# A four-layer graph network on one core: layer 0's first transfers, its softmax totals and its mark flips moved

## The reference, cut to what matters

```python
scores = jnp.einsum('hnd,hmd->hnm', q, k)
scores = jnp.where(adj > 0, scores, NEG_FILL)
attn = jax.nn.softmax(scores, axis=-1)
out = jnp.einsum('hnm,hmd->hnd', attn, vv)
...
x = _layernorm(x + _L0_gnn_ref(x, L0_gnn_x2, L0_gnn_v, adj), axis=-1)
```

## Time and profile before

| What | us |
|---|---|
| Three runs, median (lowest, highest) | 784.59 (783.59, 786.24) |
| The profiled execution's own time | 784.18 |
| Its span | 782.5 |
| TensorE busy in the span | 726.0 |
| VectorE busy | 657.7 |
| ScalarE busy | 545.3 |
| Mean granted TensorE clock, share of full | 0.984 |

### The profile page before, as it was taken

One profiled execution on the slowest core, in us unless ns is written; L12 is line 12 of the kernel. 1 busy time (PEld: TensorE's weight loads), 2 busy tenths in 40 slices (PEclk: granted clock), 3 DMA queues, 4 the chain that ended last, 5 costly groups with the idle time before them and its releaser, 6 DMA issues. The chain is left out here.

```text
span 782.5 us, 22935 instructions
## 1 busy us (share of the span) xinstructions
PE 726.0 (93%) x9908; PEld 454.3 (58%) x9908; DVE 657.7 (84%) x1001; ACT 545.3 (70%) x588; POOL 112.1 (14%) x220
## 2 busy tenths in 40 slices
PE   4798999999999999998889999999966999999996
PEld 1232333333333333336679999999963577776885
DVE  4797999999999999977899999999985757664544
ACT  7898999999999998773699999999904411111000
POOL 1421100310000000004310000000002323321222
PEclk9999999999999999999999999999996999999999
DMA  9998635363545451003271111101005000000001
GB/s 344 247 240 203 173 95 137 89 142 96 136 96 136 98 109 22 2 15 111 53 271 56 57 56 55 41 21 57 3 2 216 1 1 1 2 1 0 28 28 54
DMA packets 42599, 68.39 MB, mean 87 GB/s; under 512 B 4032, under 2 KB 27200, under 8 KB 40832
## 3 DMA queue, kind: packets, MB, share of 16 engines
q1 hardware_dynamic: 32976, 60.08, 25.3%
q0 software_dynamic: 9520, 6.82, 5.2%
HBM read 52.60 MB, written 10.09 MB: 80 GB/s over the span
## 5 line engine op out<-in xcount | busy, mean ns | idle before, releaser
L624 ACT ACTIVATE ex<-scores_ps,joint_shift 128x1024 f32<-128x1024 f32 x256 | 266.7, 1121 | 18.0 <-PE scores_ps L454 17.9
L707 DVE TENSOR_TENSOR esum<-esum,ex 128x1024 f32<-128x1024 f32 x188 | 217.2, 1216 | 1.2 <-ACT ex L624 1.2
L451 PE MATMUL scores_ps<-qst,kst 64*64 64x512 f16 x2048 | 158.7, 385 | 9.0 <-ACT ex L624 9.0
L1480 ACT ACTIVATE steps<-a_all,big_b_head 128x2048 fp8e5<-128x2048 f32 x86 | 163.6, 1988 | 0.0
L1195 PE MATMUL banks<-fx,pos 128*128 128x132 f16 x2048 | 159.4, 221 | 3.9 <-DVE pos L1387 3.7
L470 PE MATMUL mixed_total_ps<-ex,v 128*32 128x512 f32 x1024 | 125.6, 609 | 1.8 <-DMA v<-in_v_dram 1.8
L1195 PEld LDWEIGHTS banks<-fx,pos 128*128 128x128 fp8e5 x2048 | 120.6, 97 | 4.6 <-DVE pos L1387 2.6
L451 PEld LDWEIGHTS scores_ps<-qst,kst 64*64 64x64 f16 x2048 | 48.4, 106 | 116.0 <-ACT ex L624 84.7
L1202 PE MATMUL banks<-fm,edge 128*128 128x66 f16 x2048 | 103.7, 193 | 0.0
L454 PE MATMUL scores_ps<-masks,negI 64*64 64x512 bf16 x1024 | 99.8, 379 | 0.0
L1202 PEld LDWEIGHTS banks<-fm,edge 128*128 128x128 fp8e5 x2048 | 86.1, 97 | 0.0
(11 more groups left out here) (222 smaller groups left out, 722.9 us busy)
## 6 DMA issues: line engine op xcount, KB each, us to landing
adj_raw<-in_adjT_dram SPq DMA_DIRECT2D x32, 512.0 KB, 4.5
qst<-pieces_dram SPq DMA_DIRECT2D x28, 256.0 KB, 5.1
a_all<-score_rows_dram SPq DMA_DIRECT2D x7, 1024.0 KB, 6.6
edge<-masks POOLq DMA_DIRECT2D x32, 128.0 KB, 4.7
edge_copy_dram<-edge SPq DMA_DIRECT2D x1, 4096.0 KB, 17.1
edge_second<-edge_copy_dram SPq DMA_DIRECT2D x1, 4096.0 KB, 12.7
pieces_dram<-high_low SPq DMA_DIRECT2D x14, 256.0 KB, 4.2
ex<-in_x2T_dram SPq DMA_DIRECT2D x2, 1024.0 KB, 8.1
```

What stands on the lines that cost most here:

```text
L451: nc.tensor.matmul((one, two)[x][at], keys[rows, x, :], qst[rows, it % 2, half, 2 * p + x, :], start=(half == 0), stop=False, skip_group_c ...
L624: nc.scalar.activation(ex[:, slot(s), 2 * p:2 * p + 2, at], scores_ps[:, u % SR, :].rearrange("p (x n) -> p x n", n=CW), ACT.Exp, bias=joi ...
L707: nc.vector.tensor_tensor(esum[:, heads, at], other, ex[:, slot(s), heads, at], ALU.add).then_inc(summed, 1)
L1480: nc.scalar.activation(steps[:, pair_of(h, k) % SLOTS, jt % GU, :], aall[:, e, :], ACT.Relu, bias=bigh[:, e, jt:jt + 1], scale=BIG, satura ...
```

## The change

Five things. Totals: `add_halves` is gone; `total` reads the full width, eight matmuls instead of four, waits for the last additions of the round, and stands in step 8k, behind the mixing and ahead of the fourth score. Closing pieces: 0 and 1 in step 8k, 2 to 4 in the three after. Splits for later rounds: high part one step earlier, low part first in its step. Flips: all 16 behind VectorE's last additions, none in layer 1, and no waits on them there. First transfers: SP waits for the first half of `v` before x2 and x of the second group; SP's order within a step is store, load, stack; the second half of `v` comes at step 4 as one load and four swapped ones; `edge` stores begin at step 5; VectorE makes three low parts before the squares.

```diff
@@ -125,9 +125,12 @@
     JOBS = [("k", 0, 0), ("q", 0, 0), ("k", 0, 1), ("k", 0, 2), ("k", 0, 3), ("q", 1, 0), ("k", 1, 0), ("k", 1, 1),
             ("k", 1, 2), ("k", 1, 3), ("q", 0, 1), ("q", 1, 1), ("q", 0, 2), ("q", 1, 2), ("q", 0, 3), ("q", 1, 3)]
     FIRST = 5
-    SPLIT_AT = {2: 5, 3: 6, 5: 7, 7: 8, 8: 9, 9: 10, 17: 11, 25: 12, 33: 13, 41: 14, 49: 15}
+    SPLIT_AT = {2: 5, 3: 6, 5: 7, 7: 8, 8: 9, 9: 10, 16: 11, 24: 12, 32: 13, 40: 14, 48: 15}
+    LOW_AT = {s + (s >= 2 * JP): j for s, j in SPLIT_AT.items()}
     STEP_OF = {j: s for s, j in SPLIT_AT.items()}
     CONVERT_AT = {(m, t): m - 2 if m < JP else 2 * m + t - 10 for m in range(2, CONVERTED) for t in range(2)}
+    EDGE_AT = [max(m + 5, CONVERT_AT.get((m, 1), 0) + 1) for m in range(CONVERTED)]
+    SECOND_V_AT = 4
     CONVERTS = [[n for n in CONVERT_AT if CONVERT_AT[n] == s] for s in range(STEPS)]
 
     def round_of(c, g):
@@ -137,7 +140,7 @@
         what, g, c = JOBS[j]
         return JP * (round_of(c, g) - 1) - 1 if what == "q" and c else -1
 
-    STORE_AT = {j: STEP_OF[j] + 1 for j in STEP_OF}
+    STORE_AT = {j: s + 1 for s, j in LOW_AT.items()}
     STACK_AT = {j: max(STEP_OF[j], free_after(j)) + 2 for j in STEP_OF}
     LOAD_AT = {j: STEP_OF[j] - 2 for j in STEP_OF}
...
@@ -297,6 +300,7 @@
                 load_x(1)
                 for m in range(AHEAD):
                     load_adj(m)
+                sp.wait_ge(v_landed[0], 16)
                 load_x(2)
                 load_x(3)
                 for m in range(AHEAD):
@@ -309,11 +313,13 @@
                         for m, t in CONVERTS[s - 1]:
                             if t and m + AR < CONVERTED:
                                 load_adj_after(m)
-                    for j in range(3, len(JOBS)):
-                        if LOAD_AT.get(j) == s:
+                    for j in STORE_AT:
+                        if STORE_AT[j] == s:
+                            store_pieces(j)
+                    for j in LOAD_AT:
+                        if LOAD_AT[j] == s:
                             load_natural(j)
-                        if STORE_AT.get(j) == s:
-                            store_pieces(j)
+                    for j in STACK_AT:
                         if STACK_AT[j] == s:
                             stack(j)
...
@@ -349,19 +355,11 @@
                     for to, of in ((LO, HI), (HI, LO)):
                         pool.dma_start(vt[to, g, :, at], of_v[of]).then_inc(v_landed[g], 16)
 
-                def load_first_v():
-                    pool.dma_start(vt[:, 0], tiles(v)[:, :, 0:GW]).then_inc(v_landed[0], 16)
-                    pool.wait_ge(v_landed[0], 16)
+                def load_v(g):
+                    pool.dma_start(vt[:, g], tiles(v)[:, :, g * GW:(g + 1) * GW]).then_inc(v_landed[g], 16)
+                    pool.wait_ge(v_landed[g], 16)
                     for h in range(1, HG, 2):
-                        load_swapped(0, h)
-
-                def load_second_v():
-                    for h in range(HG):
-                        if h % 2:
-                            load_swapped(1, h)
-                        else:
-                            at, of = slice(h * DH, (h + 1) * DH), slice(GW + h * DH, GW + (h + 1) * DH)
-                            pool.dma_start(vt[:, 1, :, at], tiles(v)[:, :, of]).then_inc(v_landed[1], 16)
+                        load_swapped(g, h)
 
                 def keep_edges(m):
                     c, jp = m // JP, m % JP
...
-                load_first_v()
-                for m in range(AHEAD):
-                    keep_edges(m)
+                load_v(0)
                 for s in range(STEPS + 8):
-                    if s == 2:
-                        load_second_v()
-                    if 0 < s <= STEPS:
-                        for m, t in CONVERTS[s - 1]:
-                            if t:
-                                keep_edges(m)
+                    if s == SECOND_V_AT:
+                        pool.wait_ge(exp_ready, s * UNITS)
+                        load_v(1)
+                    for m in range(CONVERTED):
+                        if EDGE_AT[m] == s:
+                            if s <= STEPS:
+                                pool.wait_ge(exp_ready, s * UNITS)
+                            keep_edges(m)
                     if s == RANGE_AT + 2:
                         range_of_weights()
...
                         pe.wait_ge(shift_kept, 1)
                     if s % JP == 0 and it < G:
-                        pe.wait_ge(v_landed[it], 16 * (1 + HG, 3 * HG // 2)[it])
+                        pe.wait_ge(v_landed[it], 16 * (1 + HG))
                     for t in range(2):
                         jt = 2 * jp + t
                         for h in range(HG):
@@ -474,14 +472,16 @@
                     last.then_inc(mixed, 1)
 
                 def total(it):
-                    pe.wait_ge(halved, (it + 1) * PAIRS)
+                    pe.wait_ge(summed, (it + 1) * ADDS)
                     if it:
                         pe.wait_ge(recip_step, (it - 1) * CLOSING + 1)
                     if it == SUM_AT // JP:
                         pe.wait_ge(w_ready, KT)
-                    for h in range(HG):
-                        last = nc.tensor.matmul(total_ps[h * DH:(h + 1) * DH, :], ones[:, 0:DH], esum[:, h, 0:CW],
-                                                start=True, stop=True)
+                    for t in range(2):
+                        for h in range(HG):
+                            last = nc.tensor.matmul(total_ps[h * DH:(h + 1) * DH, :], ones[:, 0:DH],
+                                                    esum[:, h, t * CW:(t + 1) * CW], start=(t == 0), stop=(t == 1),
+                                                    skip_group_check=True)
                     last.then_inc(totals, 1)
...
                         for i in range(UNITS - 1):
                             score(s, i)
-                    if s > JP and s % JP == 1:
-                        total(s // JP - 1)
                     if s == STEPS:
                         last_total(esum, True)
                     if s:
                         mix(s - 1)
+                    if s and s < STEPS and s % JP == 0:
+                        total(s // JP - 1)
                     if s < STEPS:
                         score(s, UNITS - 1)
...
                 step = Chain(dve, top_step)
                 keep_shift(0)
-                make_low(2)
-                square(0)
-                for j in range(3, FIRST):
+                for j in range(2, FIRST):
                     make_low(j)
-                square(1)
+                for i in range(2):
+                    square(i)
 
                 def add(s, i):
                     it, jp = s // JP, s % JP
@@ -705,12 +704,6 @@
                         dve.wait_ge(summed, adds_before(it, jp - 1, i))
                         other = esum[:, heads, at]
                     nc.vector.tensor_tensor(esum[:, heads, at], other, ex[:, slot(s), heads, at], ALU.add).then_inc(summed, 1)
-
-                def add_halves(it, p):
-                    heads = slice(2 * p, 2 * p + 2)
-                    dve.wait_ge(summed, (it + 1) * ADDS)
-                    nc.vector.tensor_tensor(esum[:, heads, 0:CW], esum[:, heads, 0:CW], esum[:, heads, CW:2 * CW], ALU.add
-                                            ).then_inc(halved, 1)
 
                 def close(it, piece):
                     g, at, done = it % G, columns(it // G), it * CLOSING
@@ -784,12 +777,12 @@
                 for s in range(STEPS):
                     it, jp = s // JP, s % JP
                     for i in range(UNITS):
+                        if i == 0 and s > 2 * JP and s in LOW_AT:
+                            make_low(LOW_AT[s])
                         if jp and s < STEPS - 1:
                             add(s, i)
-                        elif not jp and it and i < PAIRS:
-                            add_halves(it - 1, i)
-                        if i == 1 and s in SPLIT_AT:
-                            make_low(SPLIT_AT[s])
+                        if i == 1 and s < 2 * JP and s in LOW_AT:
+                            make_low(LOW_AT[s])
                         if i == UNITS - 1 and s in (2, 3):
                             reduce_norms(1, s - 2)
                         if i == UNITS - 1 and s == 4:
@@ -798,8 +791,10 @@
                             step(nc.vector.tensor_reduce(out=within[:, 0:1], in_=joint[:], axis=AX.X, op=ALU.min))
                             step(nc.vector.tensor_scalar(within[:, 1:2], within[:, 0:1], -SCALE / 2 * WIDEST * WIDEST, None,
                                                          ALU.is_ge))
-                        if it and 1 <= jp <= CLOSING + 1 and i == UNITS - 1:
-                            close(it - 1, jp - 1)
+                        if it and jp <= CLOSING - 1 and i == UNITS - 1:
+                            if jp == 0:
+                                close(it - 1, 0)
```

(15 more changed lines are left out.)

9 lines of the change are left out of this document (4 added, 5 removed).

## The result

| | before | after |
|---|---|---|
| median of 4 runs each, us | 784.62 (783.59 to 786.24) | 790.63 (790.32 to 792.59) |
| ratio, 95% interval | | 1.008, 1.006 to 1.010 |
| profiled execution, us | 784.18 | 792.59 |
| its span, us; mean granted clock | 782.5; 0.984 | 790.9; 0.976 |

The forecast was 780.9, range 777.5 to 785.0, mostly faster. The change is slower by 6.0 us, 0.8%. The profiled execution of after lies 2.0 above its median, so the traces differ by 8.4 us and the medians by 6.0.

A forecast was written before the change was run, and what follows sets the result against it. TensorE and ScalarE set the pace together, 4.69 us a step; transfers set the start. First round -1.8, its seam -0.4, six seams -0.8, flips -0.7: -3.7 on 784.18, 780.5; median forecast 780.9, range 777.5 to 785.0.

The forecast's parts named there:

- The first transfers: Start of layer 0: `v` lands earlier, the adjacency pair 1.5 to 2 us late; 0 net, bounds -2.65 and +2.
- rival C: Start of layer 0: the adjacency pair comes 2 us late, the first mixing gains nothing; 782.9 us, chance 0.25.
- The natural chunk: First round: ScalarE's 1.80 us wait for the load for job 8 goes; -1.8 us, bounds -1.8 and 0.
- the low clock: Mixing of 68.12, first round's seam: 3.18 us instead of 1.92, to go with the chunk wait; -1.3, or 0.
- The second half of `v`: First round: 0.5 MB more bytes; ScalarE's later adjacency wait left at 0.5 us, bounds 0 and 1.7.
- The first round's seam: End of the first round, step 8: -1.3 for the mixing, +0.9 for the longer total; -0.4 us.
- Six seams: Rounds 2 to 7: halves -6.5, ScalarE waits -1.8, longer totals +5.2, late additions +2.3; -0.8 us, bounds -0.3 and -3.1.
- rival D: Totals of step 8k: TensorE stands for VectorE's additions, waits 10.4 us instead of 2.3; 789.0 us, chance 0.10.
- Flips: All 16 hidden under the wait for the last total, 0; four fewer in layer 1, -0.7 us, bounds 0 and -1.4.

The follow-up runs named there:

- b1: The kernel before with only SP's wait for the first half of `v` ahead of `x2` and `x3` added: median 792.38 us, ratio 1.007 to 1.012.
- e1: The changed kernel, with POOL's swapped loads of the first half of `v` held until the adjacency pair has landed: median 797.60 us, 1.012 to 1.020.
- a1: The changed kernel without SP's wait for the first half of `v` ahead of `x2`: median 783.71 us, 0.995 to 1.000 of before.
- a2: a1 with the second half of `v` loaded in its old form, in pieces, at step 2 without a wait: median 782.86 us, 0.995 to 1.000.
- c1: a1 with the second half of `v` in the new form issued at step 2 without a wait: median 782.35 us, 0.995 to 0.998.
- b4: The kernel before with only the later splits moved, halves and old totals kept: median 783.71 us, 0.996 to 1.001.
- b2: The kernel before with the new totals and closings and no halves, splits not moved: median 784.95 us, 0.998 to 1.002.
- b3: The kernel before with the new totals and closings, no halves, and the later splits moved: median 783.25 us, 0.996 to 1.000.

## Why the prediction was wrong, step by step

**The first transfers: wrong, and this is the miss.** The step that failed is "I take 0 net, bounds -2.65 and +2". The mechanism was named ("the engines run dry between `v`'s landing and the first byte of `x2`") and its sign was rival C's; the size was off. Of the landing that I estimated at 23.3, the terms: `v` at 14, measured 15.46, 1.5 late. Start, bytes and landing of `x2`, 2 and 2.5 us, measured 4.89 from its issue at 15.48 to 20.37: 0.4 late. The rest, 1.5 MB of `x3` and the first of the pair and 0.5 MB of swapped loads, which I took at the 428 GB/s of a stretch with no competing loads, 4.9 us: measured 8.78, to 29.15, at a mean of 290 GB/s. So the rate is 3.9 of the 5.85 by which the estimate was short (against the kernel before, whose engines don't stand idle there, the idle time is the largest part, 3.0 of 7.4). The time to fill empty queues is less clear: `x2` behind the hold took 4.78 us in b1 and 4.89 in after, as long as the first load of the kernel (4.83 to 5.20 in the sixteen), but 6.06 in e1, where nothing of POOL's was beside it. The Trainium skill, "DMA: Bandwidth & Descriptors", section "Anatomy of one DMA", gives some 2 us fixed beside the bytes for a load that GpSimd issues; these are SyncE's. By its rate I estimate 2.4 us for the bytes of 1 MB, 4.4 in all: the first loads and two of the three are over that by 0.4 to 0.8, that of e1 by 1.7. The upper bound of +2 should have come from the 4.1 that the same paragraph names as the most for start and landing, and from a rate under contention (251 GB/s): the 2.5 MB with the swapped half MB by 251 GB/s are 12.5 us, and from 14 with 4.1 beside them the worst case is past 30. C's own price, 2 us, was for the same reason the one that was wrong.

The other half held: the first mixing no longer waits for `v`. It gave back 1.2 of 2.65 (+7.40 at step 1, +6.18 at step 2): the mixing ran at the lower clock again, 3.36 us, and ScalarE stood 1.43 us behind it.

**The natural chunk: right.** The 1.80 is gone in every kernel with SP's new order. But the low clock that I had tied to it is not: the new wait for adjacency came in its place, and the mixing behind that took 3.21. **The second half of `v`: wrong size.** Left at a wait of 0.5, bounds to 1.7; it was 3.2 in after and 3.0 in a1, and 0.5 in a2, which issues it at 22. By bytes alone it is 0.5 MB; what I did not count is that at step 4 all of its 1.5 MB comes on top of the stacks, loads and stores of that stretch; issued at 22 the same bytes let every conversion through (c1). The question was when, and I had priced what. So the -1.8 for the first round came out as +2.0 from step 2 to 8, where a2 is 3.8 shorter than after.

**The first round's seam: right in number, and in part by luck.** Forecast -0.4, from -1.3 and +0.9, measured -0.7. b1 and b4, which have the old total in step 8 and no mixing at the lower clock there, take 11.21 and 11.18 from step 8 to 10, and after 11.53. So the slow mixing in the seam was worth 1.0 in that execution of before, and the new total costs 0.3 against kernels without it.

**Six seams: right, near in every term.** Forecast -0.8, measured -1.3. The terms are -6.5 + 5.2 + 2.3 = +1.0 for halves, longer totals and lateness, and -1.8 for the copy beside the total. b2 measured the first three alone, +1.0, and b3 minus b2 the last, -2.3. The wait for additions was 1.9, longest 1.7, where I took 2.3, mostly at the seventh total; rival D, 10.4, did not come. What I had not seen is that the copy is all of the gain, and that the old totals have room for it too (b4).

**Flips: half right.** The sixteen are hidden under the last total, whose wait falls to 1.18. The -0.7 in layer 1 did not come: the bias landed 9.88 us after the first statistics instead of 8.82, the wait that I had at 0.73 became 2.10, and the stretch took 0.7 longer, not shorter. That landing scatters from 8.75 to 10.01 in the six kernels with the flips in their old place. Where a wait for a transfer ends a row of VectorE's work, as here, work taken from ahead of it gains nothing.

**The rest.** At 63 the sum of these is +6.15, and the medians differ by 6.0. The last 1.7 us of the traces' 8.4 lie past the first use of the spread factors, in stretches in which TensorE had the lower clock for longer (0.55 granted from 587 to 607 in after, 0.66 from 580 to 600 before). That stretch takes 396.65 us before and 398.34 in after; in b2, whose code there is that of before, it takes 398.33, and in a1 and e1, whose code there is that of after, 396.5. So it comes with single executions and doesn't belong to the change.

## What to carry to other kernels

A wait that orders transfers costs what the queues fail to move once they run dry, and everything that stands behind it is late with it. A hold that ended on an earlier load, with bytes still in flight, cost nothing, but it did not bring the favoured load forward either; so look first whether that load lands earlier at all. Price what is behind the hold by the rate of a contended stretch. When you read a stage by its length, look at the stage ahead of it too: a transfer that was moved forward may have been paid for there. And where a seam is rebuilt together with a small instruction moved into it, try the small move by itself first: here 0.4 us of ScalarE in another step was nearly all the gain of the rewrite.

## What the runs showed of the hardware

Behind the hold in e1, with nothing in flight ahead of them, loads issued from 15.93 on moved 94 GB/s on the mean from 16 to 18 us and 418 from 18 to 20: two microseconds until full rate. In after, the rate fell from 393 (18 to 20 us) to 258 and 228 GB/s (22 to 26 us) while the DMA engines stayed 96% to 99% busy: a busy share near 1 said nothing of the bytes moved. And in four kernels whose code is the same up to step 8, step 2 began anywhere from 30.69 to 33.90 us in single executions, a scatter of 3.2 us, more than any part of this change was worth in the median but the hold.
